# Attention scores from two float32r parts in row halves of the array, in place of three bfloat16 parts in column quarters

## The reference

```python
# B=4 here; N is 1024 tokens; H=16 heads of 16
qkv = x @ Wqkv.T + bqkv
qkv = qkv.reshape(b, n, H, -1).transpose(0, 2, 1, 3)
q, k, v = jnp.split(qkv, 3, axis=-1)
scale = k.shape[-1] ** 0.5
scores = jnp.einsum('bhqd,bhkd->bhqk', q, k) / scale
attn = jax.nn.softmax(scores, axis=-1)
out = jnp.einsum('bhqk,bhkd->bhqd', attn, v)
out = out.transpose(0, 2, 1, 3).reshape(b, n, -1)
return out @ Wo.T + bo
```

## Time and profile before

| | us |
|---|---|
| median of 3 runs | 1917.22 |
| the profiled execution's own time | 1909.27 |
| span of its trace, first to last instruction | 1907.2 |
| projection stage | 629 to 751 |
| score stage | 751 to 1448 |

### The profile page before, as it was taken

How to read it: one execution, slowest core, us unless ns; L and a number is a source line. 1 busy time by engine, 2 the same in 40 slices (tenths; PEclk the granted TensorE clock), 3 DMA queues, 4 the chain that set the end, 5 groups by cost and what they waited for, 6 DMA issues and landing times. The chain is left out here.

```text
span 1907.2 us, 51808 instructions
## 1 busy us (share of the span) xinstructions
PE 1843.2 (97%) x19842; PEld 1434.6 (75%) x19842; DVE 1343.7 (70%) x2689; ACT 1174.8 (62%) x2387; POOL 433.1 (23%) x509
## 2 busy tenths in 40 slices
PE   7999899999999898999999999999999999999998
PEld 5788789999999664555555556555546789999997
DVE  7566678544446687999999999999944877444445
ACT  4222445444444665899998899998995644444443
POOL 4122101455552342000000000000000001555551
PEclk9999899999999999999999999999999999999999
DMA  7000111222226584312211111121005311222228
GB/s 310 1 1 0 67 53 38 66 78 78 76 78 199 134 213 131 84 51 50 48 42 42 42 42 42 42 50 34 3 3 205 102 37 32 78 78 78 72 75 270
DMA packets 86538, 148.99 MB, mean 78 GB/s; under 512 B 35748, under 2 KB 69284, under 8 KB 80612
## 3 DMA queue, kind: packets, MB, share of 16 engines
q1 hardware_dynamic: 68428, 103.11, 18.1%
q0 software_dynamic: 17856, 42.60, 8.0%
q10 hardware_dynamic: 24, 0.02, 0.0%
HBM read 96.55 MB, written 48.76 MB: 76 GB/s over the span
## 5 line engine op out<-in xcount | busy, mean ns | idle before, releaser
L2242 ACT ACTIVATE att_scores_pt<-att_scores_psE 128x512 f32<-128x512 f32 x1024 | 598.4, 598 | 68.3 <-PE att_scores_psE L1716 26.6
L1731 DVE TENSOR_REDUCE att_mx<-att_scores_psS 128x1 f32<-128x1024 f32 x472 | 577.9, 1225 | 49.7 <-PE att_scores_psS L1716 18.8
L1716 PE MATMUL att_scores_psE<-att_qs,att_ks 99*32 99x512 bf16 x4096 | 437.0, 382 | 4.3 <-DVE att_scores_psO L2272 3.5
L2344 PE MATMUL att_scores_psO<-att_scores_pt,att_va 128*17 128x256 f32 x4096 | 330.3, 379 | 2.9 <-ACT att_scores_osb L2247 1.3
L1716 PE MATMUL att_scores_psS<-att_ks,att_qs 96*32 96x512 bf16 x3776 | 308.2, 380 | 0.1
L1716 PEld LDWEIGHTS att_scores_psE<-att_qs,att_ks 99*32 99x32 bf16 x4096 | 135.7, 95 | 104.7 <-ACT att_scores_pt L2242 8.6
L2344 PEld LDWEIGHTS att_scores_psO<-att_scores_pt,att_va 128*17 128x17 f32 x4096 | 131.4, 98 | 103.2 <-issue 13.2
L865 PE MATMUL moe_ps<-W_rest,moe_srcT_high 128*128 (+2 forms) x824 | 200.4, 324 | 0.0
L658 DVE TENSOR_TENSOR moe_hidT_rest<-moe_ps,moe_hidT_high 128x384 fp32r<-128x384 f32 x142 | 79.2, 558 | 156.3 <-ACT moe_hidT_high L377 156.3
L283 POOL DMA_INDIRECT expert_rows<-work,moe_slots_i x142 | 140.0, 986 | 204.9 <-ACT work L399 179.5
L1716 PEld LDWEIGHTS att_scores_psS<-att_ks,att_qs 96*32 96x32 bf16 x3776 | 125.8, 97 | 78.1 <-issue 1.3
(11 more groups left out here) (329 smaller groups left out, 3230.8 us busy)
## 6 DMA issues: line engine op xcount, KB each, us to landing
W_gate_up<-in_gate_up_dram SPq DMA_DIRECT2D x2, 6346.0 KB, 22.5
work<-expert_rows SPq DMA_DIRECT2D x12, 1024.0 KB, 7.8
query_key_parts<-att_qkv_parts SPq DMA_DIRECT2D x64, 192.0 KB, 3.1
normalised_rows<-work SPq DMA_DIRECT2D x64, 128.0 KB, 1.8
att_qs<-query_key_parts SPq DMA_DIRECT2D x16, 384.0 KB, 4.3
att_ks<-query_key_parts SPq DMA_DIRECT2D x16, 384.0 KB, 4.4
W_down<-in_down_a_dram SPq DMA_DIRECT2D x2, 2304.0 KB, 27.9
work<-normalised_rows SPq DMA_DIRECT2D x36, 128.0 KB, 2.1
```

The costliest lines, as they stand in the source:

```text
L1716: last = nc.tensor.matmul(out[j:j + 32, :], stationary[:, j:j + 32], moving, start=True, stop=True, tile_position=(0, j), skip_group_check ...
L1731: return nc.vector.tensor_reduce(a.mx[g % 2][:, v:v + 1], bank[:, :, :].rearrange("p h k -> p (h k)"), AX.X, ALU.max)
L2242: nc.scalar.activation(pt[s % 2][:, r, :], psE[use % E_BANKS][:, :], ACT.Exp, scale=HD ** -0.5).then_inc(p_ready, 1)
L2344: last = nc.tensor.matmul(psO[32 * r:32 * r + VC, cols], va[g][:, kt, r * VC:(r + 1) * VC], pt[s % 2][:, r, cols], start=(kt == 0 and part ...
```

## The change

Queries and keys are kept in two float32r parts (high and rest) in place of three bfloat16 parts. A head now takes 48 rows (high, high, rest of the queries against high, rest, high of the keys), plus two rows for the two parts of the maximum. Two heads of a group stand in rows 0 to 63, two in rows 64 to 127. A product is one matmul of 128 stationary columns in one half of the rows (`in_rows`), not four of 32 columns. The order of a slot becomes: head 0 and the first half of unit 0 (a head of the other row half); head 1 and its second half; head 2 and the first half of unit 1; head 3 and its second half; then both parts of the sums of slot `s - 1`. `UNIT_HEADS` orders the units so that a unit's head is always in the other half of the rows. In the projection stage, units are done two at a time, side by side, once both bank pairs are free. The middle and low steps (ScalarE, GpSimd) go; ScalarE's high part and VectorE's rest are stored as float32r. A group's parts are stored by twice as many DMAs of 32 partitions, and loaded by eight DMAs (with the values nine) in place of six (seven). The maxima are split in two parts and transposed as float32. The buffers of the values move into another region.

```diff
-PARTS = 3
-PART_RUNS = [(0, PARTS, 0, 0), (3, 2, 0, 1), (5, 1, 0, 2)]
-KROWS = 6 * HD
-MROWS = KROWS + 3
+PARTS = 2
+SIDES, ROWS_OF_SIDE = 2, P // 2
+OF_SIDE = GROUP // SIDES
+RUNS = (((0, 1), (1, 2)), ((0, 2), (2, 1)))
+KROWS = 3 * HD
+MROWS = KROWS + PARTS
+ONES_FROM = ROWS_OF_SIDE // 2
+UNIT_HEADS = (2, 0, 3, 1)
...
+def rows_of(tensor, r, rows):
+
+    side, i = divmod(r, OF_SIDE)
+    return tensor[side * ROWS_OF_SIDE + rows.start:side * ROWS_OF_SIDE + rows.stop, i, :]
...
-        self.qs = [sb(f"qs{g}", [MROWS, GROUP, S], BF16) for g in range(NG)]
-        self.ks = [sb(f"ks{g}", [MROWS, GROUP, S], BF16) for g in range(NG)]
+        self.qs = [sb(f"qs{g}", [P, OF_SIDE, S], F32R) for g in range(NG)]
+        self.ks = [sb(f"ks{g}", [P, OF_SIDE, S], F32R) for g in range(NG)]
...
-LOADS = 2 * len(PART_RUNS) + 1
+LOADS = 2 * SIDES * len(RUNS[0]) + 1
...
-def by_columns(nc, out, stationary, moving):
-
-    for j in range(0, P, 32):
-        last = nc.tensor.matmul(out[j:j + 32, :], stationary[:, j:j + 32], moving, start=True, stop=True,
-                                tile_position=(0, j), skip_group_check=True)
-    return last
...
+def in_rows(nc, out, r, stationary, moving):
+
+    return nc.tensor.matmul(out, stationary, moving, start=True, stop=True, tile_position=(r // OF_SIDE * ROWS_OF_SIDE, 0),
+                            skip_group_check=True)
...
+def unit_at(v):
+
+    return v // GROUP, UNIT_HEADS[v % GROUP]
+
+
+def maximum_product(nc, a, bank, g, v, h):
+
+    q, r = unit_at(v)
+    rows = slice(0, KROWS)
+    return in_rows(nc, bank[:, h, :], r, rows_of(a.qs[g], r, rows)[:, q * P:(q + 1) * P], rows_of(a.ks[g], r, rows)[:, h * HALF:(h + 1) * HALF])
...
     nc.gpsimd.tensor_tensor(part(0), mx[:, :], a.zeros[:, :], ALU.add)
     pool.drain()
-    nc.gpsimd.tensor_tensor(a.mxr[:, :], mx[:, :], part(0), ALU.subtract)
-    pool.drain()
-    nc.gpsimd.tensor_copy(part(1), a.mxr[:, :])
-    pool.drain()
-    nc.gpsimd.tensor_tensor(part(2), a.mxr[:, :], part(1), ALU.subtract).then_inc(a.mx_ready, 1)
+    nc.gpsimd.tensor_tensor(part(1), mx[:, :], part(0), ALU.subtract).then_inc(a.mx_ready, 1)
...
-        last = nc.tensor.matmul(bank[0:GROUP * 3, q * P:(q + 1) * P],
-                                a.mx3[:, v * (QT // 2) + q, :, :].rearrange("p r c -> p (r c)"),
-                                identb[:, :], start=True, stop=True)
+        last = nc.tensor.transpose(bank[0:GROUP * PARTS, q * P:(q + 1) * P],
+                                   a.mx_parts[:, v * (QT // 2) + q, :, :].rearrange("p r c -> p (r c)").bitcast(F32), ident[:, :])
...
-                    sp.wait_ge(lo_ready, c * NM + m + 1)
-                    for i in range(P // (HD * GROUP)):
+                    sp.wait_ge(rest_ready, c * NM + m + 1)
+                    for i in range(P // (HD * OF_SIDE)):
...
                 if c == 1:
+                    sp.wait_ge(a.rows_ready, 1 + SIDES * NG)
...
-            def middle(c, m):
-                act.wait_ge(rest_ready, c * NM + m + 1)
-                nc.scalar.copy(parts[c % 2][m][:, 1, :], rest[m][:, :]).then_inc(mid_ready, 1)
...
             def maxima(c, i):
-                for n, (g, v) in early_maxima(c, i):
+                for n, (g, v) in early_maxima(c, i)[::2]:
...
-                    elif n >= 2:
-                        pe.wait_ge(a.unit_used, n - 1)
-                    maximum_products(nc, a, psS[n % 2], g, v).then_inc(a.unit_done, 1)
+                    else:
+                        pe.wait_ge(a.unit_used, n)
+                    for h in range(2):
+                        for j in range(2):
+                            last = maximum_product(nc, a, psS[j], g, v + j, h)
+                            if h == 1:
+                                last.then_inc(a.unit_done, 1)
...
-                by_columns(nc, bank[:, :], ks[g][0:MROWS, r, kt * P:(kt + 1) * P],
-                           qs[g][0:MROWS, r, half * HALF:(half + 1) * HALF]).then_inc(e_done, 1)
+                in_rows(nc, bank[:, :], r, rows_of(ks[g], r, rows)[:, kt * P:(kt + 1) * P],
+                        rows_of(qs[g], r, rows)[:, half * HALF:(half + 1) * HALF]).then_inc(e_done, 1)
...
-                    def earlier_sums(part):
+                    for r in range(GROUP):
+                        scores(b, g, s, r, first and s == 0)
+                        j, h = divmod(r, 2)
+                        for v in units[j:j + 1]:
+                            unit_half(mg, v, use, bank, h, first)
+                            if h == 1:
+                                use, bank = use + 1, 1 - bank
+                    for part in range(2):
                         if s >= 1:
                             sums(b, g, s - 1, part, first and s == 1)
                         elif not first:
                             sums(pb, pg, SLOTS - 1, part)
-
-                    for part in range(2):
-                        scores(b, g, s, 2 * part, first and s == 0)
-                        for v in units[part:part + 1]:
-                            unit(b, g, s, mg, v, use, bank, first)
-                            use, bank = use + 1, 1 - bank
-                        scores(b, g, s, 2 * part + 1, first and s == 0)
-                        earlier_sums(part)
```

125 lines of the change are left out of this document (52 added, 73 removed).

## The result

The kernel before takes 1915.94 us (median of 15 runs, 1911.36 to 1918.97), the changed kernel 1936.34 us (median of 15, 1923.35 to 1943.43): the ratio is 1.010, with a 95% interval of 1.0081 to 1.012. The change makes the kernel slower, by 20.4 us between the medians. The forecast was 1922 us on a median of 1917.2, 4.8 us more. The profiled execution of after took 1943.43 us with a span of 1941.4, the longest of its fifteen; its span is 34.2 us above the 1907.2 of before, whose profiled execution (1909.27 us) was shorter than all fifteen of before's runs here. So the 34.2 us between the two profiles overstate what the change costs. Executions over 1.5% above the fastest of their kernel are in no ratio: one of the kernel before on the chip of experiments 1 to 4 (4728.92 us) and the profiled one of experiment 10.

What follows compares the result with a forecast made beforehand. TensorE alone was taken to set the steady slot's pace at 2.604 us. Scores +8.8 and projections -4 gave +4.8 us: 1922 us on a median of 1917.2, range 1878 to 1975.

Steps and rivals of the forecast that it cites:

- the forecast case: Score slots: a chain of 2.53 to 2.64 us sets the slot; own range 1911 to 1937 us, chance 0.37.
- The matrix work: Score slot on TensorE: row halves fully overlap, so eight products cost 0.92 us in place of 1.74.
- The switches: Two tiling changes per score slot: 0.11 to 0.12 us one way, 0.08 back, plus an unhidden load; 0.30 us taken.
- The chain: Score slot through ScalarE: sums, first product, exponential, fourth product, sums; 2.58 us against 2.604, -5.7 us over 236 slots.
- The first rival: Score slots run at VectorE's pace, 2.37 us, as switches cost less; 1867 to 1911 us, chance 0.30.
- Slots without maxima: The other 20 score slots go from 2.07 to 2.58 us, since the same chain holds there: +10.2 us.
- The transposes: Once or twice a score group: maxima's 0.60 us against 0.41, +5.7 us; sums' 0.57 against 0.72, -4.6 us.
- The clock: Fourth rival: TensorE's new pauses in the scores bring back 1.2 GHz for good, +1.3 us a slot, 2250 us; chance 0.04.
- The projections: Projection stage: removed casts and paired products gain, more stores cost; -4 us taken, with -6 and +4 as ends.
- eight memsets on an idle GpSimd: Projection stage: memsets ahead of the added wait for the rows of -1 on SyncE would be done long before.
- my better end: Projection stage: the favourable end of the forecast, -6 us, where -4 was taken.
- SyncE's 128 stores: Projections: 128 part stores in place of 64, 12.8 us a chunk on SyncE's queue; +2 to +4 us if cover fails.

Runs made afterwards that it cites:

- experiments 1 to 4: The first four follow-up runs, all edits of the changed kernel, on one chip where the kernel before has a median of 1910.62 us.
- experiment 10: Changed kernel with GpSimd's memsets started only after the first four normalised tiles, run again on another chip: 1935.58 us, ratio 1.0055 to the kernel before.
- Experiment 4: Changed kernel with units' heads reordered so a maximum's product stands in the same row half as the exponentials' product before it: 1977.48 us, single run.
- Experiments 1: Changed kernel with the sums in two blocks again, one behind each pair of heads: 1896.4 us, ratio 0.9938 to the kernel before.
- experiment 7: Changed kernel with later memsets and unread products in slots without maxima, sums still at the slot's end: 1916.59 us, ratio 1.0026 to the kernel before.
- experiment 8: Kernel before (three bf16 parts, four column strips) with only its sums moved to the slot's end: 1908.6 us, ratio 0.9984 to the kernel before.
- experiment 2: Changed kernel with GpSimd's memsets started only after the first four normalised tiles: 1924.47 us, ratio 1.0096 to the kernel before.

## Why the prediction was right or wrong

The direction was right, and the median lies within the range, at the upper end of the forecast case's own (1936.34; 1911 to 1937). The sum was not right: +4.8 us was forecast, +20.4 came between the medians and +34.2 between the profiled executions. By the steps:

**The matrix work** came as put: pairs start within 0.01 us of each other, and side by side they cost one product. Experiment 4 agrees in the one product that it does put behind another, 0.22 us.

**The switches.** 0.11 was forecast one way and 0.12 came; 0.08 the other way, and again 0.12 came. The Trainium skill, "TensorEngine Tiling (Array Packing)", Tiling Modes, Key Properties, lets a change of mode drain TensorE; the trace agrees, with 0.12 us each way.

**The chain** was the right mechanism, and its size was 0.03 us short, 2.61 against 2.58, by that switch back. On 236 slots this is 7 us, and it turns the forecast gain of 5.7 into a loss of 1.4. Experiments 1, 7 and 8 show it three ways: cut, alone, and covered. The first rival, VectorE's pace with a 2.37 us slot, never came, not even with the chain cut, where TensorE with four switches needs 2.44. The chain's place in the steady slots is small in before against after, since before's own work takes 2.60 us; its price is what the same change gains with the sums in two blocks, 21 to 24 us (experiment 7).

**Slots without maxima** at the upper clock: 7.5 us more for sixteen slots, where 16 x 0.51 = 8.2 was forecast. Right.

**The transposes** came as put: a slot with a transpose of maxima takes 0.56 us more than another (0.60 forecast), one with sums' 0.58 (0.57).

**The clock** was the largest miss. I gave the lower level 0.04 and thought of it as all or nothing, for the steady slot, and argued against it with a stage whose idle time came otherwise. It came in the last group alone, where the pauses are longest and no product for a maximum fills them, and cost 14.3 us of the profiled execution (55.7 us for sixteen slots where experiment 7 has 41.4). The price that I had worked out for one slot, +1.3 us, was near: 4.04 - 2.59 = 1.45 came. The Trainium skill, "TensorE: Matmul & The Clock Gate", Part 1, A second HAM failure mode, tells of a kernel that idles shortly between groups and swings between both clocks; after's trace agrees in the last group, with 0.50 granted from 1436 to 1460 us, 0.96 from 1464 to 1468 and 0.50 behind that, and differs from it in the steady slots, with 1.00 from 900 to 1400 us. I should have asked of each kind of slot by itself what its pauses are, as I had done for its length.

**The projections.** -4 was forecast and -1.8 came. The sentence on the "eight memsets on an idle GpSimd" is the one that failed: it asked whether the memsets would be done in time for whoever waits for them, and not whose work runs beside them. They held up VectorE and cost 4.3 us. Without them the stage gains 6.7 us (124.4 to 117.6, the mean of six), a little beyond my better end of 6. The Trainium skill, "SBUF — State Buffer", Who interferes with whom, has the rule that I missed: VectorE's tensor_scalar can take a mode that needs the pair of ports that it shares with GpSimd, whichever of the two issues first keeps the pair for its whole instruction, and the other is blocked. The trace agrees in size: 7.76 / 4 = 1.94 us a tile where one memset takes 1.87, and neither the subtraction nor VectorE's small memsets beside it were slowed. Who issues first it doesn't show: the first tile's row starts 0.13 us before the first memset's (632.61 and 632.74) and lasts 2.08 us all the same. By that rule the price of this cover could have been estimated beforehand. For harm by SyncE's 128 stores the rows show no sign: sixteen of one chunk took 7.5 us (646.6 to 654.1) and not 16 x 0.65 = 10.4, and the next chunk's began 2.8 us later.

**The sum again,** with what was measured: steady groups +3.1, the start of the scores +2.1 (the lower clock there lasted longer than before, 0.59 granted on average over its first 20 us against 0.86), last group +9.7 and +14.2 for its clock, projections -1.8, and 6.9 from parts that the change doesn't touch: 34.2. The median of after contains less of the clock's part than the profiled execution does. Without the clock's 14.2 and the untouched 6.9, 13.1 us are left, and the fastest runs of the two kernels, 1923.35 and 1911.36, are 12.0 apart. That after's two fastest runs stand at 1923 and 1924 us, where the forecast for the median stood, is luck: against 4.8 us the mechanisms at the upper clock cost 12 to 13, most of it in the last groups (+9.7).

## What to carry to other kernels

When a change shrinks the work of the engine that sets the pace, draw the chain through the other engines in the same step: an order that was free (experiment 8) became the bound because the work that covered it was removed in the same change, and putting the first sums back before the third product, at the price of two more switches, turned 1.0% slower into 0.6% faster. Price the pauses that such a chain leaves by each kind of slot, for TensorE's clock can fall in the one that has least beside it. And a step on an "idle" GpSimd is not always free while VectorE runs beside it: ask what VectorE does in the meantime.

## What the runs showed of the hardware

- Two float32r matmuls in the two halves of the array's rows (50 and 48 rows, 128x512) start within 0.01 us and run side by side; pairs follow each other every 0.24 us, and after an open load after 0.34. A product in one half can start ahead of products issued before it in the other half (experiment 4: the third head's product starts at 896.48 with the first head's, the maximum's product between them at 896.82).
- Between matmuls in column quarters and matmuls in row halves there is a silence of 0.12 us, the same both ways.
- A float32 memset of 32x2048 on GpSimd takes 1.87 us and can hold a tensor_scalar of VectorE up for all of it (1.94 us a tile of 128x256 instead of 0.35), while tensor_tensor (128x512) and small memsets (128x16) ran on beside it at 0.67 and under 0.1 us.
- TensorE's granted clock fell to 0.50 in slots in which TensorE waits for ScalarE and no second product fills the wait (from 1436 to 1460 us in after, all of the last group in the longest execution of experiment 10), and stayed at 1.00 there in another execution of the same kernel (experiment 2). With a product that nothing reads in those pauses it was 1.00 in all three traces, and the kernel was faster: ratio 1.0062 instead of 1.010, and 1.0026 instead of 1.0055 to 1.0096 with the later memsets.
